# Scores of 32-row attention heads as products on 32 rows of the array, four heads at once, in a decoder kernel on one core

## The reference, cut to what matters

```python
B, S, D = x.shape
H, dk = (NUM_HEADS, D_K)          # 16 heads, width 8
Q = (x @ wq.T + bq).reshape(B, S, H, dk).transpose(0, 2, 1, 3)
K = (x @ wk.T + bk).reshape(B, S, H, dk).transpose(0, 2, 1, 3)
V = (x @ wv.T + bv).reshape(B, S, H, dk).transpose(0, 2, 1, 3)
Q, K = _rope(Q, K)
score = jnp.einsum('bhqd,bhkd->bhqk', Q, K) / jnp.sqrt(jnp.asarray(dk, x.dtype))
attn_w = jax.nn.softmax(score, axis=-1)
out = jnp.einsum('bhqk,bhkd->bhqd', attn_w, V)
```

## Time and profile before

| | |
|---|---|
| median of three runs | 421.82 us (421.66 to 422.69) |
| the profiled execution's own time | 420.76 us |
| its span, first to last instruction | 419.0 us |
| PE busy | 372.4 us (89%) |
| DVE busy | 284.1 us (68%) |
| ACT busy | 224.7 us (54%) |
| mean granted clock of TensorE | 0.982 |
| share of the chain that ended last | PE 70%, DVE 19%, issue 5% |

### The profile page before, as it was taken

How to read it: one execution, slowest core, us unless ns; L and a number is a source line. 1 busy time by engine, 2 the same in 40 slices (tenths; PEclk the granted TensorE clock), 3 DMA queues, 4 the chain that set the end, 5 groups by cost and what they waited for, 6 DMA issues and landing times.

```text
span 419.0 us, 9114 instructions
## 1 busy us (share of the span) xinstructions
PE 372.4 (89%) x3274; PEld 328.2 (78%) x3274; DVE 284.1 (68%) x840; ACT 224.7 (54%) x526; POOL 54.3 (13%) x62
## 2 busy tenths in 40 slices
PE   4688898999889999699997999999997998979791
PEld 3576776887779898689986898978996877868691
DVE  6597889888965656732687346762569898864853
ACT  2155666665766564566447564676543866551231
POOL 7700004900000000000000000000003000111124
PEclk9699999999999999899999999999999999999997
DMA  5756410214250000200010000011012022552221
GB/s 160 197 173 182 115 53 24 77 46 116 98 150 2 2 2 0 77 2 2 1 52 25 2 2 2 0 50 29 2 28 62 3 76 70 169 178 64 62 64 34
DMA packets 23644, 25.68 MB, mean 61 GB/s; under 512 B 3241, under 2 KB 18354, under 8 KB 23601
## 3 DMA queue, kind: packets, MB, share of 16 engines
q1 hardware_dynamic: 22128, 23.47, 19.3%
q0 software_dynamic: 512, 0.97, 0.7%
q10 hardware_dynamic: 960, 0.66, 0.6%
HBM read 18.35 MB, written 6.83 MB: 60 GB/s over the span
## 4 chain that ended last, share of the span: by engine, by line
PE 70%; DVE 19%; issue 5%; ACT 2%; DMA 2%; POOLq 0%; SPq 0%; POOL 0%; ACTq 0%; DVEq 0%
PE bank_D L851 13%; PE bank_C L737 10%; PE bank_D L709 9%; PE bank_A L720 7%; DVE negmax L1250 5%; PE bank_A L867 4%; PE bank_A L869 4%; PE bank_A L868 4%; PE bank_D L635 2%; PE bank_D L768 2%; PE bank_D L693 2%; PE bank_A L655 1%; PE bank_D L751 1%; PE bank_A L1586 1%; DVE q_sp L1245 1%
## 5 line engine op out<-in xcount | busy, mean ns | idle before, releaser
L1250 DVE TENSOR_REDUCE negmax<-bank_D 128x2 f32<-128x512 f32 x192 | 127.8, 685 | 38.3 <-PE bank_D L709 37.6
L997 ACT ACTIVATE expo<-bank_A 128x512 f32<-128x512 f32 x192 | 109.7, 596 | 47.7 <-PE bank_A L720 45.9
L709 PE MATMUL bank_D<-k_head,q_sp 128*128 128x256 f32 x384 | 89.0, 317 | 6.4 <-DVE negmax L1250 3.1
L720 PE MATMUL bank_A<-q_sp,k_head 128*128 128x256 f32 x384 | 81.4, 296 | 4.1 <-DVE q_sp L1245 3.9
L1033 ACT ACTIVATE hidden<-bank_A,b 128x256 f32<-128x256 f32 x128 | 53.7, 471 | 54.2 <-PE bank_A L869 54.2
L709 PEld LDWEIGHTS bank_D<-k_head,q_sp 128*128 128x128 f32 x384 | 60.3, 196 | 18.5 <-issue 8.9
L851 PE MATMUL bank_D<-mix_w,hidden 128*128 128x128 f32 x512 | 67.9, 276 | 0.9 <-DVE qk_lo L1125 0.9
L720 PEld LDWEIGHTS bank_A<-q_sp,k_head 128*128 128x128 f32 x384 | 59.6, 191 | 6.6 <-DVE q_sp L1245 5.5
L851 PEld LDWEIGHTS bank_D<-mix_w,hidden 128*128 128x128 f32 x512 | 62.6, 192 | 2.2 <-issue 2.1
L737 PE MATMUL bank_C<-expo,v_aug 128*32 128x256 f32 x768 | 46.4, 382 | 0.6 <-ACT expo L997 0.3
L1309 DVE SCALAR_TENSOR_TENSOR y_mixture<-bank_D,g_w,y_mixture 128x128 f32<-128x128 f32 x64 | 22.3, 348 | 30.3 <-PE bank_D L851 26.2
(11 more groups left out here) (188 smaller groups left out, 513.5 us busy)
## 6 DMA issues: line engine op xcount, KB each, us to landing
mix_w<-in_mix_w SPq DMA_DIRECT2D x24, 256.0 KB, 3.7
k_head<-k_scratch SPq DMA_DIRECT2D x92, 48.0 KB
k_scratch<-qk_hi SPq DMA_DIRECT2D x24, 128.0 KB, 2.4
w_last<-in_mix_w SPq DMA_DIRECT2D x8, 256.0 KB, 5.5
k_scratch<-qk_lo SPq DMA_DIRECT2D x12, 128.0 KB, 2.3
proj_w<-in_proj SPq DMA_DIRECT2D x1, 640.0 KB, 5.4
xe_scratch<-empty_row SPq DMA_DIRECT2D x1, 520.0 KB, 4.7
expo<-xe_scratch SPq DMA_DIRECT2D x2, 260.0 KB, 3.0
```

Source lines behind the costliest of these rows:

```text
L709: last = mm(where(seq, b, ("max", k))[:, qt * SEQ:(qt + 1) * SEQ], q_sps[SET[seq, b]][:, k // 4, qt * P:(qt + 1) * P], k_heads[SET[seq, b] ...
L720: last = mm(where(seq, b, ("exp", h))[:, kt * SEQ:(kt + 1) * SEQ], k_heads[SET[seq, b]][:, t, g, kt * P:(kt + 1) * P], q_sps[SET[seq, b]][ ...
L997: activate(expo[:, exp_slot(seq, b, h), :], where(seq, b, ("exp", h))[:], ACT.Exp, scale=float(HD) ** -0.5).then_inc(free(seq, b, ("exp", ...
L1250: V.tensor_reduce(negmaxes[SET[seq, b]][:, s // 4, :, 32 * (s % 4)], where(seq, b, ("max", s))[:].rearrange("p (q n) -> p q n", q=QT), AX. ...
```

## The change

The scores of a head become products over its own 32 rows: both operands are cut to partitions 32g to 32g+31. The planes of `k_heads` for the other heads go, so it shrinks to [128, group, 256], and POOL clears a quarter of what it did. The scores leave the attention steps and are made in a function `scores(tick)` of their own, at the start of every even tick, for two heads at once: first `WARM["scores"]` products of a projection by itself (only up to tick 83), then the first halves of two heads by query and two heads by key, then their second halves. Each of the four writes its own bank. The completion of a head is signalled with its second half. DVE and ACT still take one head a tick, at the start of the tick. The steps by key and all later steps of a block move by two ticks, and the starts of blocks and mixtures from tick 83 on move by 1 to 4.

```diff
-EXP_AT = 8
-VALUES_AT = 17
-BACK_AT, CTX_AT, OUT_AT, ROOT_AT, NORM_AT, TURN_AT = 26, 28, 30, 31, 32, 34
+EXP_AT = 10
+VALUES_AT = 19
+BACK_AT, CTX_AT, OUT_AT, ROOT_AT, NORM_AT, TURN_AT = 28, 30, 32, 33, 34, 36
...
-WARM = {"values": 4, "back": 3, "ctx": 4, "out": 2, "turn": 13, "logits": 2, "rank": 7}
+WARM_UNTIL = 84
+WARM = {"scores": 2, "values": 4, "back": 3, "ctx": 4, "out": 2, "turn": 13, "logits": 2, "rank": 7}
...
-             (3, SELF0, 80), (2, CROSS0, 96), (3, CROSS0, 121), (0, CROSS1, 140), (1, CROSS1, 172),
-             (2, CROSS1, 188), (3, CROSS1, 204)]
-MIXTURE = [(0, MIX0, 83), (1, MIX0, 107), (2, MIX0, 131), (3, MIX0, 156)]
+             (3, SELF0, 80), (2, CROSS0, 96), (3, CROSS0, 122), (0, CROSS1, 142), (1, CROSS1, 172),
+             (2, CROSS1, 188), (3, CROSS1, 208)]
+MIXTURE = [(0, MIX0, 85), (1, MIX0, 109), (2, MIX0, 133), (3, MIX0, 159)]
...
+def score_pairs(tick):
+
+    by_query, by_key = [], []
+    for seq, b, at in ATTENTION:
+        s = tick - at
+        if s % 2 == 0 and 0 <= s < HEADS:
+            by_query += [(seq, b, s), (seq, b, s + 1)]
+        if s % 2 == 0 and 0 <= s - EXP_AT < HEADS:
+            by_key += [(seq, b, s - EXP_AT), (seq, b, s - EXP_AT + 1)]
+    return by_query, by_key
...
-        k_heads = sets("k_head", [P, GROUPS, 4, SEQ], f32r)
+        k_heads = sets("k_head", [P, GROUPS, SEQ], f32r)
...
-                    for qt in range(QT):
-                        last = mm(where(seq, b, ("max", k))[:, qt * SEQ:(qt + 1) * SEQ],
-                                  q_sps[SET[seq, b]][:, k // 4, qt * P:(qt + 1) * P],
-                                  k_heads[SET[seq, b]][:, k // 4, k % 4, :], start=True, stop=True)
-                    last.then_inc(full(seq, b, ("max", k)), 1)
...
+                def score_by_query(seq, b, h, qt):
+                    r, t = rows_of(h), h // 4
+                    return mm(where(seq, b, ("max", h))[:, qt * SEQ:(qt + 1) * SEQ],
+                              q_sps[SET[seq, b]][r, t, qt * P:(qt + 1) * P],
+                              k_heads[SET[seq, b]][r, t, :], start=True, stop=True)
...
+                def scores(tick):
+
+                    by_query, by_key = score_pairs(tick)
+                    for one in by_query:
+                        wait_by_query(*one)
+                    if by_query and tick < WARM_UNTIL:
+                        seq, b, h = by_query[0]
+                        for _ in range(WARM["scores"]):
+                            mm(where(seq, b, ("max", h))[:, 0:P], weight("k0"), weight("k0"),
+                               start=True, stop=True)
+                    for one in by_query:
+                        score_by_query(*one, 0)
+                    for one in by_key:
+                        wait_by_key(*one)
+                    for one in by_key:
+                        score_by_key(*one, 0)
+                    for seq, b, h in by_query:
+                        score_by_query(seq, b, h, 1).then_inc(full(seq, b, ("max", h)), 1)
+                    for seq, b, h in by_key:
+                        score_by_key(seq, b, h, 1).then_inc(full(seq, b, ("exp", h)), 1)
```

More of the change, by code:

```diff
@@ L110, in beginnings, with heads_at, by_the_clock @@
     return sorted(starts)
-def by_the_clock(attention, mixture, causal, routing):
+def score_pairs(tick):
[7 more added lines that the diff above has]
+    return by_query, by_key
+def heads_at(tick, start):
+    return [(seq, b, tick - at - start) for seq, b, at in ATTENTION if 0 <= tick - at - start < HEADS]
+def by_the_clock(attention, mixture, causal, routing, scores):
     stages = {SELF0: attention, CROSS0: attention, CROSS1: attention, MIX0: mixture,
@@ L122, in by_the_clock @@
             live.append(stages[b](seq, b))
+        scores(tick)
         live = [program for program in live if next(program, live) is None]
@@ L220, in routing @@
             yield
-    by_the_clock(attention, mixture, causal, routing)
+    by_the_clock(attention, mixture, causal, routing, scores)
     return turns
@@ L712, in score_by_query @@
-                    last.then_inc(full(seq, b, ("max", k)), 1)
-                def score_by_key(seq, b, h):
-                    t, g = h // 4, h % 4
-                    if g == 0:
-                        wait_drained(pe, seq, b, ("shift", t))
-                    wait_free(pe, seq, b, ("exp", h))
-                    for kt in range(QT):
-                        last = mm(where(seq, b, ("exp", h))[:, kt * SEQ:(kt + 1) * SEQ],
-                                  k_heads[SET[seq, b]][:, t, g, kt * P:(kt + 1) * P],
-                                  q_sps[SET[seq, b]][:, t, :], start=True, stop=True)
-                    last.then_inc(full(seq, b, ("exp", h)), 1)
+                    wait_free(pe, seq, b, ("max", h))
@@ new lines, in score_by_key, with scores @@
+                def score_by_key(seq, b, h, kt):
+                    r, t = rows_of(h), h // 4
+                    return mm(where(seq, b, ("exp", h))[:, kt * SEQ:(kt + 1) * SEQ],
+                              k_heads[SET[seq, b]][r, t, kt * P:(kt + 1) * P],
+                              q_sps[SET[seq, b]][r, t, :], start=True, stop=True)
+                def scores(tick):
+                    by_query, by_key = score_pairs(tick)
+                    for one in by_query:
[11 more added lines that the diff above has]
+                        score_by_key(*one, 0)
+                    for seq, b, h in by_query:
+                        score_by_query(seq, b, h, 1).then_inc(full(seq, b, ("max", h)), 1)
+                    for seq, b, h in by_key:
+                        score_by_key(seq, b, h, 1).then_inc(full(seq, b, ("exp", h)), 1)
@@ L970, in _, with scores @@
                 bq = {CROSS0: col("bqx0"), CROSS1: 0.0}
+                def scores(tick):
+                    for seq, b, h in heads_at(tick, EXP_AT):
+                        wait_filled(act, seq, b, ("exp", h))
+                        if HEADS * ORDER[seq, b] + h >= ESLOTS:
+                            act.wait_ge(pair_done, (HEADS * ORDER[seq, b] + h - ESLOTS) // 8 + 1)
+                        activate(expo[:, exp_slot(seq, b, h), :],
+                                 where(seq, b, ("exp", h))[:], ACT.Exp, scale=float(HD) ** -0.5
+                                 ).then_inc(free(seq, b, ("exp", h)), 1)
                 def attention(seq, b):
@@ L1200, in _, with scores @@
                 bq = {CROSS0: col("bqx0"), CROSS1: 0.0}
+                def scores(tick):
+                    for seq, b, h in heads_at(tick, 0):
+                        wait_filled(dve, seq, b, ("max", h))
+                        V.tensor_reduce(negmaxes[SET[seq, b]][:, h // 4, :, 32 * (h % 4)],
+                                        where(seq, b, ("max", h))[:].rearrange(
+                                            "p (q n) -> p q n", q=QT),
+                                        AX.X, ALU.max, negate=True
+                                        ).then_inc(free(seq, b, ("max", h)), 1)
                 def attention(seq, b):
```

42 lines of the change are left out of this document (12 added, 30 removed).

## The result

The changed kernel takes **493.35 us** (median of 4 runs, 489.71 to 497.48), the kernel before 422.09 us beside it (421.66 to 422.69). The ratio is 1.165, with a 95% interval of 1.1595 to 1.1705. The prediction was 416.3 us, its range 404 to 430. It was wrong by far.

What follows compares the result with a forecast made beforehand. DVE was taken as the nearest limit in stage one and PE beside the mixtures. From 420.8 us, -2 + 0.5 - 4 + 0 = -5.5 gave 415.3; with the runs' median 1.1 us higher, 416.3 us, range 404 to 430.

Steps and rivals of the forecast that it cites:

- The group's price: PE's scores: a full group of eight products costs 0.63 us (0.24 products, 0.39 shape changes) against 0.94 to 1.36.
- a rival of its own: Score groups: the second four cannot load while the first four run, 0.11 us a group, 421 us; chance 0.05.
- Stage one: Ticks 0 to 84, DVE the limit: between 7.7 us gained and about 4 us lost; mixtures' later start loses 0.5.
- I take 2 us gained: Stage one: the amount chosen between the ends, since only DVE's 7.7 us of waiting can come back.
- Stage two: Beside the mixtures, to tick 181: cheaper groups on PE gain 3.0 to 17.3 us, taken as 4.
- a microsecond taken off PE comes back nearly whole: From 120 to 320 us, beside the mixtures: PE works 190.7 of 200 us and is the limit.
- The warming: Stage one: two warming products before each of 42 groups, 0.22 us a group, 9.3 us of PE in all.
- Stage three: After the last mixture product: 3.6 us less for fewer heads left, 3.6 us more for six later ticks; sum nothing.
- At no cost: POOL's smaller clearing of `k_heads` gains nothing, since the first scores waited for transferred keys, not for it.
- The rival of the granted clock: Attention without mixture or warming, 320 to 378 us: clock falls where nothing warms PE, 427 us; chance 0.15.
- The rival of the lockstep: Pairs run in lockstep, DVE's new waits eat PE's relief, stage two gives its 3 us: 421 us; chance 0.16.
- What would show it: Signs in the timeline: start spacing in groups, DVE waits below 7.7 us, clock 1.00 from 320 us, mixtures 4 us shorter.

Runs made afterwards that it cites:

- timetable: The kernel before with only the changed kernel's later steps by key and later starts of blocks and mixtures: 427.61 us, ratio 1.013.
- nowarm: The changed kernel without its 84 warming products (`"scores": 0` in `WARM`): 488.72 us, ratio 1.1484 to the kernel before.
- full_rows: The changed kernel, same order, banks and warming, but score products over all 128 rows with the keys' zero planes back: 480.89 us, ratio 1.1307 to the kernel before.
- narrow_alone: The kernel before in its own order, with only its score products cut to 32 rows, nothing grouped or warmed: 511.60 and 511.77 us against 425.74.

## Why the prediction was wrong, point by point

- **The group's price** was 0.63 us, and is 0.53: the 0.65 us from the start before to the start behind hold one step of 0.12 us that is not the group's. A full group saves 0.41 us where I had 0.31. Two errors nearly cancel. I took 0.12 us for each four, 0.24 in all, and called it the same as the earlier trace rows; but those rows have one four every 0.22 us, 0.058 us a product, and eight products by them are 0.46 us. That was a slip in the sum, and the second four does start 0.22 us behind the first: the two fours cost 0.44 us, not 0.24, nor the 0.31 that the prediction has as its other price. Against it I took 0.39 us for the changes of shape, and two steps of 0.22 us leave 0.1 of the 0.53. The rule named in the prediction (the Trainium skill, same page, Part 3: a load overlaps products in flight only in another row group) would have the second four wait for its loads, and the 0.22 us agree with it. They do not show it, since fours on 32 columns and all rows keep the same step. It was priced as a rival of its own, 5 us, and was not what decided.
- **Stage one, "about 4 us lost (0.2 us of new waiting in half of the 42 groups)"** as the bad end is the step that failed most. The stage lost 24.8 us, of which the later start of the mixtures, which I had at 0.5, is 2.6 (timetable). I did name the second bank that "the previous group's first head holds", and then freed it after "one maximum (0.685 us)". The diff says that DVE takes one head a tick, so the second head of every pair waits for the next tick and stands behind all of this tick's other DVE work: 2.9 us in the timeline above, not 0.685. I priced the pair against the group before it, and never asked how long a pair's own second bank stays full.
- **"I take 2 us gained" from DVE's 7.7 us of waiting.** It waits 19.9 us instead. The late signal and the joint wait are worth 18 to 19 us of the whole kernel; the prediction named both in words and gave them no term of their own.
- **Stage two, "I take 4 us gained"**, read PE alone: so many groups by so much less. It lost 32.6 us. The step "a microsecond taken off PE comes back nearly whole" holds only while PE never waits. With banks held by DVE and ACT it waits, also in the mixture (L911 for ACT's exponential, 5.8 us). I left pool A with three banks and two of them in a pair out of the account altogether.
- **The warming, "0.11 us each, so 0.22 us a group and 9.3 us".** Mis-sized by two: the eight rows are records, and a float32 product of this kind leaves two. The page has 168 records for 84 products, and `61.94 0.68 ... x4` is one group's warming. At 0.11 us a record that is 0.45 us a group and 18.7 us of PE, and with the change of shape behind it 0.61 us pass from the first record to the first score (61.94 to 62.55). Its cost to the whole kernel is 7 us (nowarm).
- **Stage three, "Sum nothing"**: 11.4 us lost. full_rows has the same stage (480.3 - 360.9 = 119.4 us against 119.3), so this is the order again, not the clock.
- **At no cost** held for POOL (54.3 to 49.1 us), which nobody waits for.
- **The rival of the granted clock** had the right effect in the wrong place, and only a part of its cause. I looked for a stretch in which PE had too little to do, from 320 to 378 us, and priced 427 us. The clock fell in every stage, 103 us at the lower level; in narrow_alone it fell at 335.6 us behind 10.6 us without any idle time of PE. What it comes to is 14.5 us in the changed kernel with the group's saving already taken off.
- **The rival of the lockstep** ("the pairs run in lockstep, new waits of DVE eat what PE gives", 421 us) was the right mechanism, given 0.16 and priced at a wash. It was taken as a way not to gain, where it is the way to lose 47 us (29 and 18).
- **What would show it.** Four starts within 0.03 us: seen. Four more 0.12 us later: 0.22, as in the earlier trace rows. The distance of 0.9 us around a group: smaller, 0.65, where the price itself would have made it 0.75. DVE's waits below 7.7 us, a clock of 1.00 from 320 us, mixtures 4 us shorter: all three false, as the text said they would be if the forecast was.

## What to carry to other kernels

Where a producer makes two buffers at once and the consumer reads one a step, the second is full for a whole step of the consumer's other work: before grouping, write down for each buffer when it is filled and when it is freed, on the consumer's queue, and take as many buffers as that needs, or let the consumer read in the same groups. A group that waits for all its buffers and signals all of them at its end costs both engines a wait each time; that was 18 us here for no instruction more. And products on a part of the array are cheaper one by one, but here they took the clock down with them, so their price has to be read from a trace of the whole kernel.

## What the runs showed of the hardware that I had not expected

- With products on 32 of 128 rows the granted clock fell even behind 10.6 us of a PE without idle time: the mean is 0.826 for the kernel before with nothing changed but the rows (0.982 without), 0.894 against 0.974 between the changed kernel and the same on all rows. At the lower level everything on PE is slower, the mixtures too. This is from after at 266 us, products 0.21 us apart instead of 0.118:

```profile
266.79 0.41 PE L911 MATMUL bank_A<-x_hi,w_hi 128*128 128x256 f32 x1
267.00 0.41 PE L912 MATMUL bank_A<-x_lo,w_hi 128*128 128x256 f32 x1
267.21 0.41 PE L913 MATMUL bank_A<-x_hi,w_lo 128*128 128x256 f32 x1
```

- Four products on different row groups start within 0.01 us of each other, also with 128 columns each, but the four behind them start 0.22 us later, nearly twice the 0.118 us step of a product on the whole array, and the same as fours on 32 columns have the earlier trace rows. From the start before to the start behind them, eight in two fours passed 1.06 / 0.65 = 1.6 times as fast, not four.
- A product of 128x128 by 128 columns in float32 (the warming: 168 records for 84 products) is two records and 0.22 us, so rows counted by "x" are not always products.
